# Layer 3's attention in a four-layer kernel: key tiles worked off in fours in place of twos

## What is computed

```
q = ln(x, lnq) @ Wq + bq      k = ln(x, lnk) @ Wk + bk      v = ln(x, lnv) @ Wv + bv     (16 heads of 64)
scores = q k^T / sqrt(128) + mask        p = softmax(scores)        att = p v
h = att @ Wo + bo + x     y = ln(h)      out = gelu(y @ W1 + b1) @ W2 + b2 + h
```

## Time and profile before

| | us |
|---|---|
| median of 3 runs (lowest to highest) | 5166.38 (5153.54 to 5170.76) |
| the profiled execution: time, and span of the profile | 5170.1, 5168.8 |
| layer 3's attention, first to last values | 3736 to 5108 |

### The profile page before, as it was taken

How to read it: one execution, slowest core, us unless ns; L and a number is a source line. 1 busy time by engine, 2 the same in 40 slices (tenths; PEclk the granted TensorE clock), 3 DMA queues, 4 the chain that set the end, 5 groups by cost and what they waited for, 6 DMA issues and landing times. The chain is left out here.

```text
span 5168.8 us, 68806 instructions
## 1 busy us (share of the span) xinstructions
PE 4542.4 (88%) x27376; PEld 2215.6 (43%) x27376; DVE 3147.9 (61%) x4176; ACT 2499.2 (48%) x3813; POOL 2318.8 (45%) x1323
## 2 busy tenths in 40 slices
PE   5999999977886777858799999978799999999997
PEld 3444444445654333323322222224455555555554
DVE  4656565636765777752477777843465665565663
ACT  2344444436663555642266666652244444445443
POOL 0455555558771577870100000000066666666675
PEclk8999999989997999979799999988799999999998
DMA  1000000011110000000000000000000000000000
GB/s 32 3 3 3 3 3 3 3 29 32 37 28 12 2 2 2 1 5 19 3 2 2 1 2 1 1 9 1 10 3 3 3 1 3 3 3 1 3 1 9
DMA packets 61954, 36.81 MB, mean 7 GB/s; under 512 B 36308, under 2 KB 53888, under 8 KB 61376
## 3 DMA queue, kind: packets, MB, share of 16 engines
q1 hardware_dynamic: 61632, 32.41, 2.5%
HBM read 22.03 MB, written 1.05 MB: 4 GB/s over the span
## 5 line engine op out<-in xcount | busy, mean ns | idle before, releaser
L795 DVE TENSOR_REDUCE L_part<-banks 128x2 f32<-128x1024 f32 (+2 forms) x1600 | 1881.5, 1189 | 965.7 <-PE banks L646 825.0
L780 ACT ACTIVATE L_weights<-banks 128x1024 f32<-128x1024 f32 (+1 forms) x1600 | 1581.1, 1001 | 1056.4 <-PE banks L678 816.1
L704 PE MATMUL banks<-L_weights,L_V 128*32 128x512 f32 (+3 forms) x6400 | 1490.3, 602 | 3.6 <-ACT L_raw L729 1.8
L1002 POOL TENSOR_TENSOR L_wsum<-L_wsum,L_weights 128x1024 f32<-128x1024 f32 (+1 forms) x448 | 995.0, 2221 | 55.8 <-ACT L_weights L780 3.0
L985 POOL TENSOR_TENSOR L_wsum<-L_wsum,L_two 128x1024 f32<-128x1024 f32 x240 | 571.0, 2379 | 841.6 <-DVE L_two L969 838.5
L704 PEld LDWEIGHTS banks<-L_weights,L_V 128*64 128x64 f32 (+1 forms) x6400 | 282.3, 122 | 453.5 <-issue 397.0
L678 PE MATMUL banks<-L_QH,L_KH 64*128 64x512 f32 (+3 forms) x1664 | 432.0, 453 | 17.9 <-issue 10.2
L2513 POOL MEMSET F_xr<- 128x16 f32 x1 | 0.1, 127 | 933.4 <-POOLq L97 933.4
L646 PE MATMUL banks<-L_KH,L_QH 64*128 64x512 f32 (+3 forms) x1664 | 372.5, 429 | 31.7 <-ACT L_weights L780 17.5
L678 PE MATMUL banks<-L_QL,L_KH 64*128 64x512 f32 (+3 forms) x1664 | 372.0, 382 | 0.0
L678 PE MATMUL banks<-L_QH,L_KL 64*128 64x512 f32 (+3 forms) x1664 | 371.7, 381 | 0.0
(11 more groups left out here) (446 smaller groups left out, 5911.7 us busy)
## 6 DMA issues: line engine op xcount, KB each, us to landing
F_early<-F_V SPq DMA_DIRECT2D x63, 128.0 KB, 2.3
F_tab<-xpos SPq DMA_DIRECT2D x8, 512.0 KB, 4.4
F_h<-L_ffn_h_w SPq DMA_DIRECT2D x2, 1024.0 KB, 8.0
F_wqkv<-L_ffn_wqkv SPq DMA_DIRECT2D x2, 768.0 KB
L_cos<-rope_cos SPq DMA_DIRECT2D x1, 1024.0 KB, 5.0
L_sin<-rope_sin SPq DMA_DIRECT2D x1, 1024.0 KB, 7.0
out<-X SPq DMA_DIRECT2D x1, 1024.0 KB, 5.1
F_z<-F_x SPq DMA_DIRECT2D x32, 31.8 KB
```

What stands on the lines that cost most here:

```text
L704: mm = pe.e.matmul(O[r, c:BANK], self.V[g % 2][:, kt, h, :], self.W[x % self.NW][:, y, c:BANK], start=kt < starts, stop=kt >= tiles - starts)
L780: act.e.activation(self.W[x % self.NW][:, :, c:BANK], self.banks(it)[:, :, c:BANK], ACT.Exp, scale=self.scale).then_inc(self.exped, 1)
L795: dve.e.tensor_reduce(self.part[n % 3][:, pr, j, p, :], self.banks(it)[:, :, 0:wide], AX.X, ALU.max).then_inc(self.mx_read, 1)
L1002: pool.e.tensor_tensor(acc[:, :, c:BANK], acc[:, :, c:BANK], W[:, :, c:BANK], ALU.add).then_inc(self.summed, 1)
```

## The change

For layer 3 alone (`FOUR`), the list is made four steps at a time. A turn is: four scores four steps ahead, each followed by a quarter of the pieces, then the shift, the first half of the y-products (rounded down), the values of four steps, and the other y-products. `LEAD` goes from 2 to 4, the buffers of weights from 6 to 8. `share` counts in fours, the fetch comes at step 8 of a group and not 10, and den and the joins come 4, 8 and 8 steps behind the last turn of a chunk, both joins in one turn.

```diff
@@ class Attention
+    FOUR = False
@@ def after(self, n):
+        if self.FOUR:
+            return [(4, ("den", n)), (8, ("join", n, 0)), (8, ("join", n, 1))]
@@ def plan(self):
-        share = lambda count, left: -(-count // max(1, left // 2))
-        for x in range(0, steps, 2):
+        U = 4 if self.FOUR else 2
+        share = lambda count, left: -(-count // max(1, left // U))
+        for x in range(0, steps, U):
...
-            if x == start + 10 and g + 1 < self.groups:
+            if x == start + (8 if self.FOUR else 10) and g + 1 < self.groups:
...
-                take = max(share(sum(1 for m, it in left if m <= m0), self.first(m0 - 1) - 4 - self.LEAD - x) for m0 in {m for m, it in left})
+                take = max(share(sum(1 for m, it in left if m <= m0), self.first(m0 - 1) - 2 * U - self.LEAD - x) for m0 in {m for m, it in left})
...
-                made[it[1], it[2], it[3]] = x + (0 if self.EAGER else 2)
+                made[it[1], it[2], it[3]] = x + (0 if self.EAGER else U)
...
-                take = max(share(sum(1 for m, it in left if m <= m0), self.first(m0) - 2 - self.LEAD - x) for m0 in {m for m, it in left})
+                take = max(share(sum(1 for m, it in left if m <= m0), self.first(m0) - U - self.LEAD - x) for m0 in {m for m, it in left})
...
-            while shifts and shifts[0][1] < x and x >= self.first(shifts[0][0] - 1) - 2 - self.LEAD:
+            while shifts and shifts[0][1] < x and x >= self.first(shifts[0][0] - 1) - U - self.LEAD:
...
-            if self.APART:
+            if self.FOUR:
+                cut = len(ys) // 2
+                for i in range(4):
+                    items += [("score", soon + i)] if soon < steps else []
+                    items += ps[len(ps) * i // 4:len(ps) * (i + 1) // 4]
+                    items += carried if i == 0 else []
+                items += turns + eager(ys[:cut]) + [("values", x + i) for i in range(4)] + mid + eager(ys[cut:])
+            elif self.APART:
...
-            if k == self.chunk[n][2] - 2:
+            if k == self.chunk[n][2] - U:
@@ class NormedAttention(WideAttention):
-    EAGER = True
+    EAGER, FOUR = True, True
+    LEAD, NW = 4, 8
```

## The result

The changed kernel takes 5208.41 us (median of 5 runs, 5200.56 to 5214.23) against 5166.38 of the kernel before; the ratio is 1.0086, with a 95% interval of 1.0064 to 1.0107. It is slower, by 42 us, where 23 us were forecast. The lines after `plan` stand 13 or 14 further down in its profile: scores L691, pieces L659, values L717, den L914, join L727, exponential L793, maxima L808, division L936, low part L1199, `two` L982, GpSimd's sums L998, L1010 and L1015.

The account below looks back on a forecast made before the run. TensorE's queue was taken to bound the kernel. Terms -19 - 1 + 45 + 6 - 12 + 2 + 2 = +23 us gave 5193 for the profiled execution and 5189 us for the median, 0.45% slower; range 5135 to 5225.

Parts of the forecast that it names:

- Plain turn, -19 us: Layer 3's turns of four: fewer changes of kind against more waits for banks, 9.09 us a turn, net -19 us.
- - 1: The 6 turns where no pieces are left: some 1 us more saved.
- +6 for joins: First join ahead of the values in 17 chunks: +0.2 for each of 31 chunks, +6 us, bounds 0 to 12.
- +2 for the start: Ramp at the start, where 8 pieces fall in a turn and VectorE's 1.23 a piece is the bound: +2 us.
- 28 waits of y-products, +45: Two y-products behind the values on bank 7: TensorE waits until it is read, 14 x (1.7 + 1.5) = +45 us.
- The fetch, -12: The 7 waits at the weights' arrival: a longer turn hides 6.15 us for loads and scaling, -12 us.
- GpSimd and VectorE, +2: In 17 chunks GpSimd meets the first join ahead of its sums, 0.5 late, some 0.1 reaching TensorE: +2 us.
- the collision: Rival: GpSimd and VectorE collide as in layer 1, `two` 0.51 longer, adds 0.25: +24 to +61 on top, 5225; chance 0.14.
- the shorter chain (turn of 8.96): Rival: the bank chain in a turn is shorter, turn 8.96, net -36, so +6 in all, 5172; chance 0.25.
- the turn without waits (8.39): Rival: four scores and pieces don't wait beyond the natural 8.39, -85, so 5104; chance 0.16, cases between counted.
- That lead and buffers cost nothing: Weights' buffers and lead: weights must be free four steps behind in both orders, GpSimd having as much time as before.

Follow-up runs that it names:

- turns of four with spread y-products: Changed kernel with den 8, joins 12 and 16 steps behind a chunk, shift moved, third Wo buffer, weights' wait at the next group's first projection: 5143.83 us, ratio 0.9957.
- the later arrival: Kernel before, with layer 3's arrival one turn of two later (step 14 for 12), the fetch where it was: 5161.97 us, ratio to before 0.9995.
- the spread version: Changed kernel with den 8, joins 12 and 16 steps behind a chunk, shift between second and third score, third Wo buffer: 5158.78 us, ratio to before 1.0002.
- the version with the add moved: Changed kernel, but GpSimd alone takes a join standing ahead of the values behind that turn's four sums: 5183.43 us, ratio to before 1.0045.
- the version with neither kind of wait: Changed kernel with den, joins and shift in places of their own, and TensorE's weights' wait at the next group's first projection: 5143.83 us, ratio 0.9957.
- turns of two and the same wait: Kernel before, with TensorE waiting for loads and scaling at the next group's first projection in layer 3: 5153.98 us, ratio to before 0.9975.
- both joins in one turn: Kernel with spread y-products and the wait at the first projection, den left at 8, both joins 12 steps behind the chunk: 5178.95 us, ratio to before 1.0043.
- the version where only they were left: Kernel with spread y-products and the wait at the first projection, but den 4 steps behind the chunk again, beside Q: 5164.89 us, ratio to before 1.0002.
- half the maxima: Changed kernel, but in layer 3 VectorE takes the maxima over half of the keys only: 5173.36 us in a single execution.

## Why the prediction was right, and where not

**The sign and the main terms held; the sum came out at +23 where +42 was measured** (+40 in the stage).

*Plain turn, -19 us with its first edge:* right, start by start. By experiment, turns of four with spread y-products gain 9.0 us in the stage; the prediction's own terms for that version are -19 - 1, +6 for joins and +2 for the start, so -12. (The Trainium skill, TensorEngine Tiling (Array Packing), "Key Properties", says that a change of tiling mode drains TensorE. The trace agrees as far as it shows: from a piece to work of another tiling pass 0.31 to 0.34 us where a pair follows a pair after 0.23; the drain itself no row shows.)

*28 waits of y-products, +45:* right in number and place. den's cost 22.8 us measured alone (predicted 14 x 1.7 = 24). The joins' 17.3 us of idle stand against 14 x 1.5 = 21 with the restart; their cost alone was not separated from GpSimd's and the clock's.

*The fetch, -12:* the amount is right and the reason was wrong, so that it came out is luck. The prediction wrote that in the longer turn "6.15 us for loads and scaling are hidden". Not the loads' time counts, as the later arrival showed, but that TensorE's wait stands directly behind the score whose exponential ScalarE makes before the scaling. In the changed kernel the values of four steps (3.58 us) happen to lie between the scores and the arrival, and so the wait is gone. In the spread version a join stood there, whose division came ahead of the scaling, and the wait was back.

*GpSimd and VectorE, +2:* **the term that was mis-sized.** The prediction placed GpSimd's add of the early join rightly ("I find it 0.5 late, of which some 0.1 reaches TensorE"), but took 2 x 2.4 us for its sums and 1.24 for `two`, and ended there. The 0.5 us brings the sums and `two` together; then they cost 5.7 and 3.1 us, and the exponential waits. Moving that one add gave 17.9 us in the stage, about 11 for the turns and 3 at the end, the other 4 being the clock's. The text had the collision as a rival, at 24 to 61 us more and with a chance of 0.14, by layer 1's example; what happened, 14 us, lies between the forecast and that rival. It costs time only behind early joins: `two` also takes 1.6 to 2.0 us three times a group in the version with the add moved, where no exponential waits. By the prediction's own words, "I am wrong if [...] ScalarE's exponentials wait for GpSimd (L1002) by more than a few us in all", this part was wrong: they wait 31.9 us.

*The start, +2:* up to the first values the stage takes 9.0 us more (61.0 against 52.0), since 23 pieces and not 17, and more scores, stand there. The last group and the end are shorter for it, by 9.3 us in the version with neither kind of wait (156.5 against 165.8 with turns of two and the same wait). The prediction had only 2 us of this at the start, and nothing at the end.

*The end, not in the sum:* the last den waits 7 us longer for GpSimd (12.1 against 5.1). That den stands 4 steps behind the chunk is not the cause: there it waits 6.8 us when the joins are apart, but 10.5 with both joins in one turn, and 9.2 in the changed kernel with the add moved. So GpSimd ends its sums later for the joins' place. Nothing is left there that TensorE could do meanwhile, and the prediction didn't look at the end of the stage.

*The clock, not in the sum:* 3 falls in the profiled execution, 4 us.

With measured sizes: -12 (arrival) - 9 (turns, joins, start) + 23 (den) + about 20 (joins' waits) + 11 + 3 (GpSimd, turns and end) + 4 (clock) = about +40, against 39.9. Two of these are worked out rather than measured alone: the joins' 20 and the 11. From the experiments alone it is -12 - 9 + 23 + 29 (both joins in one turn, with GpSimd's part and without the clock's) + 4 = +35; the last 5 us of the 39.9 they don't separate.

*The rivals:* the shorter chain (turn of 8.96) and the turn without waits (8.39) fell with the plain turn at 9.09. That lead and buffers cost nothing held.

## What to carry to other kernels

A longer turn saves changes of kind only if everything that went into the gaps of the old one finds a place: two products on one bank in one turn wait for the whole reading in between, and on the engine that bounds the kernel that wait was paid in full here (22.8 us for 21.9 of idle). Once one engine's queue is late by half a microsecond, don't price the delay alone: look at what it then runs beside. And put a wait where its data are used, not where they are announced: one line moved gave 12 us here, more than turns of four did.

## What the hardware showed that was not expected

The granted clock fell to 0.5 for some 3 us behind a pause of only 1.2 us, with joins (64x128 matmuls) on either side, though TensorE was busy for 96% of the group; and behind a join and a pause of 1.56 us. Elsewhere in the same stage pauses of 1.56 us (between Q and den) did nothing in the version where only they were left. What decides behind such a pair of joins is open: the pause is 1.23 us in all of them, and the clock fell 12 times in 14 in one version and 3 times in 14 in another. Two other versions have the same list for TensorE as that last one: with GpSimd's add moved it never fell, with half the maxima 12 times. Each count is of one execution. `two` and GpSimd's adds, 1.24 and 2.39 us apart from each other, took up to 3.13 and 5.71 (for two) when they met.
